# Two narrow attentions: the exponential taken head by head on ScalarE, the division moved to the outputs

## The reference, cut to what matters

```python
# third layer
energy = jnp.einsum('nqhd,nkhd->nhqk', q, k)
energy = jnp.where(mask == 0, jnp.float32(-1e+20), energy)
attention = jax.nn.softmax(energy / np.sqrt(EMBED).astype(np.float32), axis=3)
out = jnp.einsum('nhql,nlhd->nqhd', attention, v).reshape(N, q_len, EMBED)
return out @ Wo.T + bo
# fourth layer
scores = jnp.einsum('bhqd,bhkd->bhqk', Q, K) / math.sqrt(D_K)
attn = jax.nn.softmax(scores, axis=-1)
out = jnp.einsum('bhqk,bhkd->bhqd', attn, V)
out = out.transpose(0, 2, 1, 3).reshape(b, sd, d)
return out @ Wo + bo
```

## Time and profile before

| | |
|---|---|
| median of 3 runs | 3230.22 us (3229.81 to 3231.99) |
| the profiled execution | 3223.1 us, its span 3221.9 us |
| PE busy | 3030.5 us, 94% of the span |
| DVE busy | 2136.4 us, 66% |
| ACT busy | 1223.1 us, 38% |
| POOL busy | 848.5 us, 26% |
| granted clock of TensorE, mean | 0.981 of full speed |

### The profile page before, as it was taken

The page is one execution under the profiler, slowest core; times in us unless marked ns, Lnnn a source line. Parts: engine busy times, 40 slices in busy tenths (PEclk is TensorE's granted clock), DMA queues, the critical chain, the costliest instruction groups (busy, mean ns, idle before and its releaser), DMA issues.

```text
span 3221.9 us, 43511 instructions
## 1 busy us (share of the span) xinstructions
PE 3030.5 (94%) x16352; PEld 2224.4 (69%) x16352; DVE 2136.4 (66%) x3877; ACT 1223.1 (38%) x2350; POOL 848.5 (26%) x1286
## 2 busy tenths in 40 slices
PE   7999999999999999999999999789998898997996
PEld 5678877667767776777699999556666664555664
DVE  5996879567855885686478887783218777764113
ACT  4343332553355335432233333331224346562331
POOL 1306500100110020001246655440343222111554
PEclk9999999999999999999999999999999999998998
DMA  5200100010002000200032221003451011112633
GB/s 137 67 1 1 29 27 1 13 42 27 1 14 68 0 1 14 67 1 1 14 92 79 81 91 53 20 1 105 179 196 36 5 50 51 32 41 106 215 125 108
DMA packets 104614, 176.42 MB, mean 55 GB/s; under 512 B 27125, under 2 KB 75799, under 8 KB 99671
## 3 DMA queue, kind: packets, MB, share of 16 engines
q1 hardware_dynamic: 89527, 102.32, 10.2%
q0 software_dynamic: 14880, 71.33, 6.2%
HBM read 198.31 MB, written 17.56 MB: 67 GB/s over the span
## 4 chain that ended last, share of the span: by engine, by line
PE 76%; DVE 13%; ACT 4%; issue 3%; POOL 2%; DMA 1%; SPq 0%; DVEq 0%; ACTq 0%; POOLq 0%
PE psum L419 9%; PE psum L442 8%; PE psum L1392 7%; PE psum L1404 6%; PE psum L2516 6%; PE psum L1866 5%; PE psum L1821 5%; PE psum L2537 3%; PE psum L409 2%; PE psum L455 2%; PE psum L1113 2%; PE psum L2692 2%; PE psum L727 2%; PE psum L3117 2%; DVE psum L3375 1%
## 5 line engine op out<-in xcount | busy, mean ns | idle before, releaser
L419 PE MATMUL psum<-Vt,shared 128*128 128x256 f32 (+1 forms) x1600 | 361.6, 381 | 0.4
L442 PE MATMUL psum<-Kt,xnTt 128*128 128x512 f32 (+1 forms) x960 | 343.9, 508 | 0.5 <-ACT xnTt L527 0.5
L419 PEld LDWEIGHTS psum<-Vt,shared 128*128 128x128 f32 (+1 forms) x1600 | 297.8, 190 | 39.3 <-issue 1.2
L442 PEld LDWEIGHTS psum<-Kt,xnTt 128*128 128x128 f32 x960 | 179.9, 190 | 158.0 <-issue 153.1
L1404 PEld LDWEIGHTS psum<-expert_w,prep 128*128 128x128 f32 x1024 | 194.6, 190 | 77.6 <-issue 57.4
L245 POOL TENSOR_SCALAR root_v<-meanvar 128x8 f32<-128x8 f32 (+3 forms) x19 | 8.6, 454 | 903.8 <-DVE meanvar L223 903.8
L1404 PE MATMUL psum<-expert_w,prep 128*128 128x256 f32 x1024 | 240.8, 379 | 0.0
L1392 PE MATMUL psum<-weights,expert_w 128*128 128x512 f32 x512 | 240.3, 593 | 0.0
L3375 DVE CUSTOM_DVE_ANT_0 psum<-psum,expert_w 128x128 f32<-128x128 f32 (+7 forms) x256 | 191.4, 775 | 70.0 <-PE psum L3117 66.7
L1318 DVE SCALAR_TENSOR_TENSOR bias<-Kt,small,bias 128x1232 f32<-128x1232 f32 x96 | 149.1, 1553 | 129.8 <-ACT Kt L1302 128.6
L620 DVE TENSOR_REDUCE row<-shared 128x16 f32<-128x1232 f32 x112 | 160.5, 1433 | 81.7 <-ACT shared L536 70.0
(11 more groups left out here) (509 smaller groups left out, 6617.9 us busy)
## 6 DMA issues: line engine op xcount, KB each, us to landing
weights<-in_L_ffn_w SPq DMA_DIRECT2D x32, 512.0 KB, 4.7
expert_w<-in_L_ffn_w SPq DMA_DIRECT2D x32, 512.0 KB, 4.6
expert_w<-in_L_xattn_Wf SPq DMA_DIRECT2D x16, 512.0 KB, 6.0
weights<-q_parts SPq DMA_DIRECT2D x32, 144.0 KB
weights<-k_parts SPq DMA_DIRECT2D x96, 48.0 KB
weights<-in_L_xattn_Wk SPq DMA_DIRECT2D x4, 1024.0 KB, 4.9
weights<-in_L_xattn_Wv SPq DMA_DIRECT2D x4, 1024.0 KB, 7.0
weights<-in_L_xattn_Wq SPq DMA_DIRECT2D x4, 1024.0 KB, 5.4
```

What stands on the lines that cost most here:

```text
L419: ins = pe.matmul(o_bank(t), probT[0:rows, t % 2, c, :], Vt[0:rows, t // TB, c, :], start=(c == 8), stop=(c == 7))
L442: ins = pe.matmul(flat[:, par * 3 * BANK + at:par * 3 * BANK + at + cols], xnTt[:, par, k, :], Kt[:, t // TB, k, src:src + cols], start=(k ...
```

## The change

In both attentions:

- `power` becomes 16 exponentials of 128x77, one for each head. Each takes the head's negated maximum from `row` as its bias, and writes the sum of its results to `row` (`accum_out`). In the second attention it reads the scores straight from PSUM.
- DVE no longer adds the maximum (L615) nor sums (L620). `shifted` is signalled by the maximum; after `powered` only the reciprocal follows. `dve_softmax` stays as it was for the wide attentions.
- The scale of the softmax moves into the keys (`KEY_SCALES`), a second operation in an instruction that is there already, and into the mask.

In the first attention, besides, what the second had already:

- POOL's multiplication of 1232 columns (L982) is replaced by the spreading of the reciprocals to 256 columns.
- PE's turning waits for `powered` instead of `weights_made`, and turns the shares of the tile before with two more transposes; ACT copies them; at the end, one set of each for the last tile.
- The copy of the weighed values on ACT (L833) becomes the multiplication on DVE, after the maximum of every other tile.

The core of the diff:

```diff
     def pe_turn_probabilities(pe, n, t):
         g, base = NT * n + t, t % 2 * 3 * BANK
-        if n == 6:
-            pe.wait_ge(powered, g + 1)
-        else:
-            pe.wait_ge(weights_made, g + 1)
+        pe.wait_ge(powered, g + 1)
...
-            if n == 6 and t >= 1 and b0 + 4 >= CH:
-                ins = pe_turn_shares(pe, t - 1)
+            if t >= 1 and b0 + 4 >= CH:
+                ins = pe_turn_shares(pe, n, t - 1)
...
+    def dve_shares(dve, n, t, src, after_maximum):
+
+        g, par = NT * n + t, t % 2
+        negmax, shares, total = (row[:, par, i * H:(i + 1) * H] for i in range(3))
+        dve.tensor_reduce(negmax, src, AX.X, ALU.max, negate=True).then_inc(shifted, 1)
+        after_maximum()
+        dve.wait_ge(powered, g + 1)
+        if t >= 2:
+            dve.wait_ge(weights_made, g - 1)
+        dve.reciprocal(shares, total).then_inc(shares_made, 1)
...
         if feed:
             pe_tables(pe)
-        else:
-            pe_turn_shares(pe, NT - 1).then_inc(p_turned, 1)
+            pe.wait_ge(xt_fed, 2)
+        pe_turn_shares(pe, n, NT - 1).then_inc(p_turned, 1)
         weigh(PAIRS - 1)
...
-        def keep_outputs(u):
-            act.wait_ge(weighed, g0 + 2 * u + 2)
-            act.copy(outT[:, :, :].rearrange("p g c -> p (g c)"), weighed_bank(u)).then_inc(outputs_kept, 1)
...
         def power(t):
             act.wait_ge(shifted, g0 + t + 1)
-            act.activation(prob[:, t % 2, :], prob[:, t % 2, :], ACT.Exp, scale=scale).then_inc(powered, 1)
+            par = t % 2
+            src = prob[:, par, :] if biased else flat[:, par * 3 * BANK:par * 3 * BANK + HK]
+            for h in range(H):
+                of_head = slice(h * S2, (h + 1) * S2)
+                ins = act.activation(prob[:, par, of_head], src[:, of_head], ACT.Exp, bias=row[:, par, h:h + 1],
+                                     accum_out=row[:, par, 2 * H + h:2 * H + h + 1])
+            ins.then_inc(powered, 1)
...
+            def after_maximum():
                 before(t)
                 if biased:
+                    if t % 2 == 0 and t >= 4:
+                        divided_outputs(t // 2 - 2)
                     if t + 2 < NT:
                         dve_normed(dve, n, x, t + 2)
...
-            if n == 5:
-                pool.wait_ge(shares_made, NT * (n - 5) + t + 1)
-                pool.tensor_tensor(Pb, Pb, shares.to_broadcast([P, H, S2]), ALU.mult).then_inc(weights_made, 1)
...
-            ins = dve.tensor_scalar(dst[:, g, :], bank[:, i * CTX:(i + 1) * CTX], add, None, ALU.add)
+            ins = dve.tensor_scalar(dst[:, g, :], bank[:, i * CTX:(i + 1) * CTX], add, (KEY_SCALES[n], 1.0)[i], ALU.add, ALU.mult)
```

More of the change, by code:

```diff
@@ L668, in build, with wide_shares, shares_T, tiles_turned @@
     HD = D // H
-    wide_shares = prep[:, 8704:9216].rearrange("p (n h c) -> p n h c", n=2, c=HD)
-    shares_T = prep[:, 7680:8704].rearrange("p (n g i q) -> p n g i q", n=2, g=KD, i=2)
+    def wide_shares(n):
+        at = flat_V1[:, 3840:4352] if n == 5 else prep[:, 8704:9216]
+        return at.rearrange("p (n h c) -> p n h c", n=2, c=HD)
+    def shares_T(n):
+        at = flat_V1[:, 2816:3840] if n == 5 else prep[:, 7680:8704]
+        return at.rearrange("p (n g i q) -> p n g i q", n=2, g=KD, i=2)
+    def tiles_turned(n, t):
+        return 3 * (NT * n + t) + n - 5
     def shares_bank(t):
@@ L814, in pe_attention, with act_attention @@
             pe_stay_at_work(pe, psum[:, 1, :], 6)
-    def act_attention(act, n, scale, q_bias=None, feed=False):
+    def act_attention(act, n, biased, q_bias=None, feed=False):
         g0 = NT * n
@@ L845, in keep_probabilities @@
                     ins = act.copy(dst[0:LASTROWS, t % 2, CH - 1, :], flat[0:LASTROWS, base + (CH - 1) * P:base + CH * P])
-                    if not feed and t >= 1:
+                    if t >= 1:
                         ins = keep_shares(t - 1)
@@ L882, in act_attention @@
                     act_feed_copy(act, i)
+        act.wait_ge(p_turned, tiles_turned(n, NT) + 1)
+        keep_shares(NT - 1).then_inc(p_kept, 1)
         if feed:
-            keep_outputs(PAIRS - 1)
             for i in range(2, FEED_PAIRS):
                 act_feed_copy(act, i)
-        else:
-            act.wait_ge(p_turned, 3 * (g0 + NT) + 1)
-            keep_shares(NT - 1).then_inc(p_kept, 1)
     def dve_attention(dve, n, biased, gate, before, after, feed=False):
@@ L902, in divided_outputs @@
             dve.wait_ge(weighed, g0 + 2 * u + 2)
-            dve.wait_ge(p_kept, 3 * (g0 + 2 * u + 2) + (3 if u < PAIRS - 1 else 1))
+            dve.wait_ge(p_kept, tiles_turned(n, 2 * u + 2) + (3 if u < PAIRS - 1 else 1))
             dve.tensor_tensor(outT[:, :, :].rearrange("p g c -> p (g c)"), weighed_bank(u),
-                              shares_T[:, u % 2, :, :, :].rearrange("p g i q -> p (g i q)"), ALU.mult).then_inc(outputs_kept, 1)
+                              shares_T(n)[:, u % 2, :, :, :].rearrange("p g i q -> p (g i q)"), ALU.mult).then_inc(outputs_kept, 1)
         def statistics(t):
@@ L934, in after_shift @@
                         residual(t - 4)
+                    if t == NT - 1:
+                        divided_outputs(PAIRS - 2)
                     if t % 2 == 0 and t >= 6:
@@ L957, in dve_attention @@
         for u in range(PAIRS - 3 if biased else PAIRS - 2, PAIRS):
-            if not biased:
+            if not biased or u == PAIRS - 1:
                 divided_outputs(u)
@@ L977, in pool_attention @@
             par = t % 2
-            Pb = prob[:, par, :].rearrange("p (h c) -> p h c", h=H)
             shares = row[:, par, H:2 * H].unsqueeze(2)
-            if n == 5:
-                pool.wait_ge(shares_made, NT * (n - 5) + t + 1)
-                pool.tensor_tensor(Pb, Pb, shares.to_broadcast([P, H, S2]), ALU.mult).then_inc(weights_made, 1)
             pool.wait_ge(normed, NT * n + t + 1)
             pool.tensor_tensor(x[:, t, :], x[:, t, :], gated_bo, ALU.add).then_inc(bo_added, 1)
[L985 to L989, removed]
+            pool.wait_ge(shares_made, NT * (n - 5) + t + 1)
+            if t >= 2:
+                pool.wait_ge(p_turned, tiles_turned(n, t))
+            pool.tensor_copy(wide_shares(n)[:, par, :, :], shares.to_broadcast([P, H, HD])).then_inc(weights_made, 1)
             if after:
@@ L2050, in narrow @@
                 dve.wait_ge(shared_head_landed, 96)
-                dve.tensor_scalar(bias[:, :, :], mask_i, 0.0, -1e20, ALU.is_equal, ALU.mult)
+                dve.tensor_scalar(bias[:, :, :], mask_i, 0.0, -1e20 / 16.0, ALU.is_equal, ALU.mult)
             elif s == 25:
```

36 lines of the change are left out of this document (14 added, 22 removed).

## The result

The changed kernel is slower: 3256.27 us median of 4 runs (3253.51 to 3258.54) against 3231.10 of the kernel before on the same chip (3229.81 to 3233.16), a ratio of 1.009 with a 95% interval of 1.0076 to 1.0105. The forecast was 3240 us in a range of 3222 to 3292.

The account below looks back on a forecast made before the run. DVE was taken to bound the first attention and PE the second. Terms 8.4 - 2.9 + 0 + 3 + 1.5 gave +10 us, from a median of 3230.2 to 3240 us, range 3222 to 3292.

Parts of the forecast that it names:

- c: Both attentions, ACT: start-to-start time of one 77-column exponential with its sum, forecast 0.32 us from SBUF and 0.26 from PSUM.
- r: Both attentions, ACT: what the sum adds to each exponential; taken as 0.05 us, between 0 and 0.24.
- the first loop: First attention: DVE and ACT take turns, 16c + 3.2 = 8.3 us a tile against 7.74, +8.4 us over 15 tiles.
- The forecast case: Whole kernel: r of 0.05 us, about +10 us; range of this case 3233 to 3255 us, chance 0.40.
- the rival of the whole record: Both attentions: read-out costs its whole 0.14 us, ACT becomes the bound; +53 us, 3283 us; chance 0.24.
- the second loop: Second attention: ACT's 16c + 0.1 + 2.55 = 6.9 us, just below PE's 7.01 and 7.33, so 0 in the middle.
- my sum: Both attentions: first's loop +8.4 and start -2.9, second's middle 0, start +3 and last tile +1.5, together +10 us.
- the end of the first attention: First attention's end: set by PE feeding the next block, so a change of 0.
- the clock: TensorE: with PE idler the granted clock may dip oftener; a danger on top, not counted in the forecast.
- my ends of 0 and 0.24: Limits for the sum's price: 0 if read-out is free, 0.24 us if its record and the overlap are lost.
- In both ACT looks free: Both attentions before the change: ACT busy 13.2 and 16.0 of 30 us, so taken as not the bound.
- the case of a free pointer: Both attentions: pointer costs nothing from start to start, c some 0.1 us less, PE sets pace; -12 us, 3218 us; chance 0.08.

## Why the prediction was right, and where it was off

**Direction and mechanism held.** The forecast was slower, by DVE and ACT taking turns in the first attention and ACT's own queue against PE in the second. Both loops are there, the first shown by moving one order and by changing c twice.

**The term that was mis-sized is r, the price of the sum.** I took 0.05 us; it is 0.09. With 0.27 for the exponential (0.25 measured) c came to 0.32 where 0.342 is true, and in PSUM to 0.26 where 0.300 is. The formulas with the true c give 16 x 0.342 + 3.2 = 8.67 us for the first loop, exactly as measured, and 7.45 for the second, measured 7.56: the records there grow from 0.36 to 0.39 us within a tile, so that the last ends some 0.1 us later than my 0.10 allowed. The forecast case ended at 3255 us, the result is 3256, between it and the rival of the whole record (3283). That rival named the point from which ACT becomes the bound of the second attention, r of 0.06, and it was passed. By it the second loop is 0.4 us above PE's mean of 7.17, which is 6 us that I had at 0. With the true c and nothing else changed my sum would have been 14.0 - 2.5 + 5.9 + 3.7 + 2.2 = +23 us, against +25 by the medians: the price of the sum is most of what was off. That this lands so near is in part luck, as two things that I had at 0, the end of the first attention and the clock, below, pull in opposite ways.

**Why 0.05 was the wrong row.** I took ACT's price of an instruction without columns for one that follows another copy. The DVE row had pulled in the same direction: there the next instruction starts with the read-out. On ACT it does not; the next exponential starts 0.09 us after the read-out did (2098.01, 2098.10). The middle between my ends of 0 and 0.24 would have been about as near to the truth as the row I chose.

**Smaller slips.** "In both ACT looks free" was too simple: in the first attention DVE waited about 0.3 us in each tile for the exponential (the 11.7 us above). PE's own pace there, which I had added up to 7.3 us from the lengths of its groups, is 6.96, since the groups overlap (the scores are 2.36 us long, and the next group starts 2.2 us after they do). And the start of the case of a free pointer, -5.3 us, leaves out the 0.05 for the sum that the forecast has; with it it is -4.5.

The Trainium skill's page "ScalarE: Activation LUTs" (What ACT_TABLE_LOAD costs) gives an ACTIVATE with a pointer 280 ns plus 0.833 ns a column, less 93 ns where two follow: 344 and 251 ns for 77 columns. The trace agrees to the nanosecond with the first (344) and with 0.25 us from start to start where the sum is left out. The budget of its rules, 0.36 us without overlap, was by chance close to what the head costs with its sum, for a reason that the page does not have.

**The ends of the attentions.** The first's start gave -2.4 us (forecast -2.9), the second's start +4.4 (+3), its end +1.4 (+1.5). The end of the first, which I had put at 0 because PE sets it, was longer: from the last turning but one to the last 16.1 us, 11.5 before. At the last but one nothing stands between the turning and the weighing, so that PE waits 2.40 us for the residual behind DVE's mask and maximum (1.55 before), and after it runs at the lower clock (8 matmuls in 3.75 us; 1.97 before). How much of the 4.6 us belongs to the change is open: the same instructions of the first attention took 13.4 us where only the second was whole again, so 2.7 us of it come and go from one run to another. With DVE's new order and the sums on DVE it is 14.0.

**The clock.** I had added as a danger that an idler PE would be granted less. In the middle of the first attention the opposite was seen: 1.00 at 60.4 busy us of 86 (70%), and not one of the dips of before, where two tiles of the same stretch took 8.8 us. That took back some 3 us of the loss, if the dips of the one trace of before are typical of it; the runs do not say why they are gone.

## What to carry to other kernels

Cutting one wide instruction into sixteen pays a fixed price sixteen times, and each operand that it gets has its own: here 0.09 us for the pointer and 0.09 for the accumulator, so that sixteen sums taken "for free" cost as much as the pass that they replace. Before an engine's work is lengthened, look at what stands behind the wait for it on the next engine: what doesn't need the result (here the next tile's mask and maximum) belongs ahead of the wait, and only then does a lighter pass turn into time. And before filling a gap, check that what is put there is ready at that time.

## What the runs showed of the hardware

- ScalarE's accumulator is read by an instruction of its own, with a record of 0.187 us (median, from SBUF), which adds 0.09 us from start to start; VectorE's has a record of 0.14 us beside which the next instruction starts.
- Source in PSUM against SBUF: 0.04 us less from start to start for 77 columns, with or without the sum (0.300 and 0.342, 0.21 and 0.25); it was measured with results that go to SBUF in both.
- Where such pairs follow each other from PSUM, the records grow through the sixteen (0.316 to 0.413 us) while the starts stay 0.300 apart: the mean duration of a group overstates what one costs.
